# A transformer layer in three blocks: q and k of the cross-attention made transposed and packed through DRAM, two heads a step, joints filled with preparation

## The chip, the cores and the metric

One core of a Trainium2 chip. The metric is the device time of one execution in microseconds (us); several executions of each kernel give a median. One execution was also recorded by the hardware profiler. The engines are TensorE (PE, matrix products and transposes), VectorE (DVE), ScalarE (ACT), GpSimd (POOL) and SyncE (SP, which here only issues DMAs). PE writes PSUM, whose banks hold 512 fp32 words per partition.

## The reference

All in fp32, x of 8 batches of 256 rows and 512 columns. Each of three blocks adds to x a function of its layernorm.

```python
x = x + _L0_attn_ref(_layernorm(x, axis=-1), L0_attn_wqkv, L0_attn_wg, L0_attn_wo, L0_attn_gn_weight, L0_attn_gn_bias)
x = x + _L0_xattn_ref(_layernorm(x, axis=-1), ctx_1024, fside_BxSx2_0, fside_BxSx2_0, L0_xattn_Wq, ...)
x = x + _L0_ffn_ref(_layernorm(x, axis=-1), L0_ffn_gate_w, L0_ffn_expert_fc1, ...)
# block 1, retention: 8 heads of 64
scores = einsum('bhid,bhjd->bhij', xpos(q), xpos(k)) * decay
y = group_norm(einsum('bhij,bhjd->bhid', scores, v))
out = (g * tanh(softplus(g))) * y @ wo.T          # g = x @ wg.T
# block 2, cross-attention: 32 heads of 16, context 256 rows of 256
q, (k, v) = x @ Wq, split(ctx @ Wkv);  q, k = axial_rope(q, pos), axial_rope(k, pos)
out = softmax(q k^T / 4) v @ Wout + bout
# block 3, feed-forward
probs = softmax(x @ gate_w.T)                      # 8 experts, top 2
y = sum over the two experts of p * (silu(x @ fc1.T) * (x @ fc2.T)) @ proj.T            # 352 hidden
y = y + sigmoid(x @ shared_gate.T) * (silu(x @ s1.T) * (x @ s2.T)) @ shared_proj.T      # 1408 hidden
```

## The kernel before

The blocks run one after another; x stays in SBUF as `X`, 16 tiles of 128 rows. Names of tiles begin with a_, b_ or c_ by block. An fp32 product is made of three products of rounded parts (`matmul3`, L41 to L43): every operand is split into a high part (a rounded copy, mostly on ACT) and a low part (the rest, a subtraction on DVE or POOL).

**Retention** (`retention`) is a pipeline over 8 batches, written out as `body(b, ...)` for every engine. PE's body makes the scores and values of batch b and, between them, the eight chunks of products of batch b + 1 (`gemm_chunk`); chunks 6 and 7 are the gate, with rows in the partitions. The mish of the gate is transposed on PE (L261, 8 a body) and multiplied by the normalised values into z (L410), whose parts enter the output product. The product with `blk` (L251) joins the group statistics. In the last body there are no products of a next batch beside this chain.

**Cross-attention** (`cross_attention`) handles one head in a step, T = 33 steps a batch, several batches live at once: LAGS and LAGV say how many steps a head's logits and values come behind its rows. q and k are made with rows in the partitions ("r"), rotated on DVE (L873) and POOL (L1071), and written with their high and low parts into `qs`, 64 columns a head: for q high, high, low and for k high, low, high, and further columns for the maximum. 64 transposes a batch (L797, "t") turn them, and DVE (L878) and ACT (L997) copy them to qT and kT: two heads in the 128 partitions, 64 each. A head then goes: `rows` (L730, two products), row maximum on DVE (L888), every eighth head the negated maxima (L902), transposed (L801), copied, and moved by small DMAs into qT (L712); `logits` (L742), exp on ACT (L1028), every four heads `values` (L755), a copy (L1022), the turn (L762), and the division on DVE (L910, L913). Rows have two banks of rt and logits two, one head each. Then the output is transposed (L806), multiplied by Wout and added (L884). The block's start loads and splits three pieces of weights, makes the rotation's angles, and clears `qs`, `vp` and `nm` on POOL while DVE normalises the first rows (L850).

**Feed-forward** (`feed_forward`) first makes the statistics (L1371) and normalises (L1382) on DVE in four groups of four tiles, transposes (L1653), and makes the router's logits (L1672). The shared branch has 11 pieces of 128 hidden columns and four groups, 44 steps: `up(n)`, 24 products of 512 columns, and two steps later `down(n)`, 12 products, whose result DVE adds to X (L1480). SP loads pieces as they come free and fills both row tables in DRAM with zeros (L1254); beside the branch the top two are chosen, rows are ranked and scattered by indirect DMAs (L1288). Then 39 tiles of rows sorted by expert: load, transpose (L1716), two products up, the hidden values turned (L1743), one product down, rows out. POOL gathers each token's rows, first choices while the last tiles run (`early`), second ones after them (`late`, L1307), and DVE adds them (L1558).

Each engine's order is written out; semaphores alone tie the engines together.

## Time and profile before

| | us |
|---|---|
| runs | 1725.29, 1719.75, 1698.67; median 1719.75 |
| profiled execution | 1727.18, span of its instructions 1725.4 |
| PE busy | 1480.3 |
| DVE, ACT, POOL busy | 945.3, 548.5, 491.1 |
| mean granted clock of PE | 0.933 of full speed |

Busy time is the union of an engine's instructions over the whole span. The blocks have different limits, so the shares of the span say less than those of a stage. Retention ends at 382.4 us, cross-attention at 977.5, and the experts' tiles at 1687.4.

### The profile page before, as it was taken

How to read it: one execution, taken by the hardware profiler on the slowest of the kernel's cores; microseconds unless marked ns; L12 is line 12 of the kernel's file. 1: busy time of each engine (PE TensorE's matmuls, PEld its weight loads, DVE VectorE, ACT ScalarE, POOL GpSimd, SP SyncE). 2: the span in 40 equal slices, each digit the busy share in tenths (PEclk: the TensorE clock that was granted, in tenths of full speed). 3: DMA queues.
4: the chain of work that ended last, by engine and by line, in shares of the span. 5: the costliest groups of instructions: out<-in, count | busy, mean ns of one | idle time of the engine just before them, and what ended most of it. 6: DMA issues, size and time to landing. Idle time of an engine off the chain costs nothing. (4 is left out here: it accounts for less than half of the span.)

```text
span 1725.4 us, 24524 instructions
## 1 busy us (share of the span) xinstructions
PE 1480.3 (86%) x8506; PEld 1157.7 (67%) x8506; DVE 945.3 (55%) x1715; ACT 548.5 (32%) x954; POOL 491.1 (28%) x341
## 2 busy tenths in 40 slices
PE   6899999944888888888889559999999999999970
PEld 4677777733556656656665347888887879999960
DVE  5566666555676676665655375655556542222215
ACT  3222222203365565555556222111111112232310
POOL 1122222124222212212120130354124157447034
PEclk9999999966799999989889679999999999999985
DMA  6000000011000000000000390123200033353246
GB/s 262 1 1 0 0 0 0 1 36 56 2 9 2 7 7 1 7 7 1 7 1 3 112 394 34 62 102 110 79 24 31 13 128 126 132 183 126 87 122 207
DMA packets 37285, 107.05 MB, mean 62 GB/s; under 512 B 4832, under 2 KB 5984, under 8 KB 34912
## 3 DMA queue, kind: packets, MB, share of 16 engines
q1 hardware_dynamic: 30944, 71.48, 11.6%
q0 software_dynamic: 6272, 34.61, 5.6%
q8 instruction: 48, 0.79, 0.2%
q14 instruction: 21, 0.17, 0.0%
HBM read 62.30 MB, written 43.25 MB: 61 GB/s over the span
## 5 line engine op out<-in xcount | busy, mean ns | idle before, releaser
L1028 ACT ACTIVATE b_pf<-b_rt,b_zero 128x512 f32<-128x512 f32 x256 | 172.3, 686 | 139.0 <-PE b_rt L742 135.4
L888 DVE TENSOR_REDUCE b_mx<-b_rt 128x2 f32<-128x512 f32 x256 | 174.2, 687 | 63.5 <-PE b_rt L730 62.6
L1480 DVE SCALAR_TENSOR_TENSOR residual<-c_yp,c_shared,residual 128x512 f32<-128x512 f32 x176 | 127.4, 745 | 142.4 <-PE c_yp L43 136.6
L730 PE MATMUL b_rt<-b_kT,b_qT 64*128 64x256 f32 x512 | 120.3, 342 | 23.5 <-DVE b_mx L888 23.4
L41 PE MATMUL c_fc<-c_xh,c_w 128*128 128x512 f32 x352 | 137.1, 390 | 0.0
L43 PE MATMUL c_fc<-c_xh,c_w 128*128 128x512 f32 x352 | 137.0, 389 | 0.0
L42 PE MATMUL c_fc<-c_xl,c_w 128*128 128x512 f32 x352 | 137.0, 389 | 0.0
L730 PEld LDWEIGHTS b_rt<-b_kT,b_qT 64*128 64x128 f32 x512 | 74.2, 197 | 74.8 <-DVE b_mx L888 40.6
L742 PE MATMUL b_rt<-b_qT,b_kT 64*128 64x256 f32 x512 | 114.8, 322 | 9.7 <-DMA b_qT<-b_mT 9.1
L41 PE MATMUL a_gemm<-a_wh,a_xl 128*128 128x512 f32 x256 | 110.2, 430 | 4.6 <-DVE a_xl L312 3.9
L41 PE MATMUL c_fc<-c_ring,c_xTl 128*128 x312 | 105.8, 339 | 4.8 <-DVE c_xTl L1485 4.8
L1578 ACT ACTIVATE c_s<-c_fc 128x512 f32<-128x512 f32 x44 | 26.3, 598 | 239.8 <-PE c_fc L43 234.3
L42 PE MATMUL a_gemm<-a_wl,a_xh 128*128 128x512 f32 x256 | 102.5, 400 | 0.0
L43 PE MATMUL a_gemm<-a_wh,a_xh 128*128 128x512 f32 x256 | 102.4, 400 | 0.0
L42 PE MATMUL c_fc<-c_ring,c_xTh 128*128 x312 | 101.5, 325 | 0.0
L43 PE MATMUL c_fc<-c_ring,c_xTh 128*128 x312 | 101.3, 325 | 0.0
L1494 DVE TENSOR_TENSOR c_hTl<-c_eh,c_hTh 128x384 fp32r<-128x384 f32 x39 | 21.7, 558 | 145.0 <-ACT c_hTh L1602 134.8
L797 PE MATMUL b_gm<-identity,b_qs 128*128 128x128 f32 x512 | 83.8, 315 | 7.4 <-POOL b_qs L1080 7.1
L1071 POOL TENSOR_TENSOR b_rr<-b_ac,b_bs 128x256 f32<-128x256 f32 x32 | 23.4, 731 | 234.0 <-DVE b_bs L873 233.8
L742 PEld LDWEIGHTS b_rt<-b_qT,b_kT 64*128 64x128 f32 x512 | 75.9, 195 | 16.8 <-DMA b_qT<-b_mT 11.2
L1282 POOL TENSOR_TENSOR c_w<-c_wraw,c_zero 128x1536 fp32r<-128x1536 f32 x11 | 30.4, 2761 | 195.1 <-DMA c_wraw<-in_c_ws 123.8
L797 PEld LDWEIGHTS b_gm<-identity,b_qs 128*128 128x128 f32 x512 | 65.9, 161 | 25.0 <-issue 19.5
(274 smaller groups left out, 3524.8 us busy)
## 6 DMA issues: line engine op xcount, KB each, us to landing
c_eraw<-in_c_we POOLq DMA_DIRECT2D x8, 2176.0 KB, 10.0
c_xe<-c_rows_in SPq DMA_DIRECT2D x39, 256.0 KB, 3.1
c_rows_out<-c_ye SPq DMA_DIRECT2D x39, 256.0 KB, 2.0
c_rows_in<-c_xe SPq DMA_DIRECT2D x19, 512.0 KB, 9.9
c_rows_out<-c_xe SPq DMA_DIRECT2D x19, 512.0 KB, 9.9
c_wraw<-in_c_ws SPq DMA_DIRECT2D x11, 768.0 KB, 4.4
a_raw<-in_a_w SPq DMA_DIRECT2D x5, 1024.0 KB, 5.7
out<-residual SPq DMA_DIRECT2D x16, 256.0 KB
```

The source lines that it names most:

```text
L41: nc.tensor.matmul(out, ll, rh, start=start, stop=False)
L42: nc.tensor.matmul(out, lh, rl, start=False, stop=False)
L43: return nc.tensor.matmul(out, lh, rh, start=False, stop=stop)
L730: last = nc.tensor.matmul(rt[:, h % 2, t * S:(t + 1) * S], qT[r:r + 64, m, t * P:(t + 1) * P], kT[r:r + 64, m, :], start=True, stop=True)
L742: last = nc.tensor.matmul(rt[:, 2 + h % 2, j * S:(j + 1) * S], kT[r:r + 64, m, j * P:(j + 1) * P], qT[r:r + 64, m, :], start=True, stop=True)
L797: last = nc.tensor.transpose(out[:, m * P:(m + 1) * P], qs[:, which, t, c:c + P], ident[:, :])
L888: nc.vector.tensor_reduce(out=mx[:, :, h], in_=rt[:, h % 2, :].rearrange("p (t s) -> p t s", s=S), op=ALU.max, axis=AX.X).then_inc(mx_done, 1)
L1028: nc.scalar.activation(pf[:, h % 8, :], rt[:, 2 + h % 2, :], ACT.Exp, scale=XD ** -0.5, bias=zero[:, :]).then_inc(e_done, 1)
L1071: nc.gpsimd.tensor_tensor(rr[:, :, 0:8], ac[:, 0, :, :], bs[:, 1, :, :], ALU.subtract)
L1282: nc.gpsimd.tensor_tensor(w[:, k, 0, :], wraw[:, k, 1, :], zero[:, :].to_broadcast([P, PW]), ALU.add).then_inc(wh_done, 1)
L1480: nc.vector.scalar_tensor_tensor(out=X[:, t, :], in0=yp[:, (n * 4 + k) % 3, :], scalar=shared[:, t:t + 1], in1=X[:, t, :], op0=ALU.mult, o ...
L1578: nc.scalar.activation(s[:, n % 2, :], fc[:, n % 2, 0, :], ACT.Silu).then_inc(s_done, 1)
```

## The change

- **Retention.** The gate is made transposed (weights are the stationary operand, 256 columns move), so mish is not transposed. `transpose_q` stands ahead of the wait for the group statistics. In the last body the weights Wq and Wkv of the next block are loaded and split, and the table of the rotation is made and turned by 32 transposes (`turn_table`). SP writes the constant rows of `pack` and the zeros of the row tables in this block.
- **Cross-attention.** q and k are made transposed, in two halves, rotated there, and SP writes their high and low parts to the DRAM tensor `pack` and reads them back (`chunk`) into kT and qT with 50 rows a head. `qs`, its 64 transposes and 16 copies a batch are gone. A step handles two heads, T = 16: their rows fill both banks, and so do the logits; maximum and exp work on 1024 elements. The maxima are turned in the values' bank. POOL copies the values to `vp`. Each batch ends with the statistics of its final rows for the next block (`final_first`, `final_statistics`).
- **Joint to the feed-forward.** In the last body of cross-attention the first two shared pieces and the router's weights are loaded and split, and four tiles are normalised and transposed (`lead_turn`). The other twelve are normalised on ACT between the first steps.
- **Feed-forward.** The last 8 of 44 `down` are held: their hidden values are kept, their parts are made beside the expert tiles (`pair_high`, `pair_low`), and `held_down` runs behind the experts, two pieces summed in PSUM, with 16 more additions on DVE. The early gathers wait for each other, two in flight. Loads of the first rows wait for the ninth piece.

The core of the diff (some lines between the parts shown are left out):

```diff
+                if c >= 6:
+                    for m in range(2 * (c - 6), 2 * (c - 5)):
+                        o = 3 * C + m * P
+                        for k in range(KT):
+                            last = matmul3(nc, bank[:, m % 2 * S:(m % 2 + 1) * S], (wh[k][:, o:o + P], wl[k][:, o:o + P]),
+                                           (xh[:, k, :], xl[:, k, :]), k == 0, k == KT - 1)
+                    last.then_inc(gemm_done, 1)
+                    return
...
+            def turn_table():
+                pe.wait_ge(csr_done, 1)
+                for g in range(B):
+                    if g >= 2:
+                        pe.wait_ge(tab_read, g - 1)
+                    for k in range(2):
+                        for t in range(TB):
+                            last = nc.tensor.transpose(tp[:, g % 2 * 2 + k, t * P:(t + 1) * P], csr[:, k, g * TB + t, :], ident[:, :])
+                    last.then_inc(tab_mm, 1)
...
+                if nxt:
+                    transpose_q(b + 1)
+                else:
+                    turn_table()
                 pe.wait_ge(gst_done, b + 1)
                 nc.tensor.matmul(sc[:, 0, 0:2 * KT], blk[:, :], gm[:, :, :], start=True, stop=True).then_inc(gmm_done, 1)
                 if nxt:
-                    transpose_q(b + 1)
                     gemm_chunk(b + 1, 5, False)
                     transpose_k(b + 1)
                     gemm_chunk(b + 1, 6, False)
-                pe.wait_ge(mish_done, b + 1)
-                pe.wait_ge(gmm_read, b + 2)
-                for t in range(TB):
-                    for k in range(KT):
-                        last = nc.tensor.transpose(sc[:, k // 2, k % 2 * S + t * P:k % 2 * S + (t + 1) * P],
-                                                   mish[:, 2 * t + k // 2, k % 2 * P:(k % 2 + 1) * P], ident[:, :])
-                last.then_inc(tm_done, 1)
                 if after:
                     transpose_x(b + 2, False)
                 if nxt:
...
-                dve.wait_ge(tm_done, b + 1)
-                nc.vector.tensor_tensor(z[:, :, :], y[:, :, :], sc[:, :, :].rearrange("p a (b s) -> p (a b) s", s=S), ALU.mult)\
+                dve.wait_ge(mish_done, b + 1)
+                nc.vector.tensor_tensor(z[:, :, :], y[:, :, :], mish[:, :, :], ALU.mult)\
...
+            sp.wait_ge(pads, 4)
+            for which in range(2):
+                for g in range(B):
+                    sp.dma_start(pack_dram[g, which, 3 * XD:3 * XD + 2, :, :, :].rearrange("r h c (a s) -> (r h c a) s", a=TB),
+                                 fix[:, which, :]).then_inc(fix_out, 16)
+            for n in range(SLOTS):
+                for rows in row_tables:
+                    sp.dma_start(rows[n * P:(n + 1) * P, :], zero_dram).then_inc(filled, 16)
+            sp.wait_ge(gemm_done, 8 * B)
+            for n in range(2):
+                sp.dma_start(raws[:, n, :], wb_dram[1 - n, :, :]).then_inc(next_in[n], 16)
+            sp.wait_ge(fix_out, 32 * B)
...
+            def next_weights():
+                act.wait_ge(ang_done, 1)
+                for n in range(2):
+                    act.wait_ge(next_in[n], 16)
+                    nc.scalar.copy(slots[1 - n], raws[:, n, :]).then_inc(next_done, 1)
+                for k in range(2):
+                    last = nc.scalar.activation(csr[:, k, :, :].rearrange("p t (i h) -> p (t i) h", h=16),
+                                                ang[:, k, :].rearrange("p (n o) -> p n o", o=1).to_broadcast([P, NT * 8, 16]), ACT.Sin)
+                last.then_inc(csr_done, 1)
+                for g in range(B):
+                    act.wait_ge(tab_mm, g + 1)
+                    nc.scalar.copy(table[:, :, g * S:(g + 1) * S], tp[:, g % 2 * 2:g % 2 * 2 + 2, :]).then_inc(tab_read, 1)
...
-        T, LAGS, LAGV = 33, 13, 18
-        NORM, CONTEXT, ROWS = -T, 17 - T, {0: 15 - T, 1: 18 - T, 2: 21 - T, 3: 24 - T}
...
+        T, LAGS, LAGV = 16, 8, 11
+        PLAN = [(32, "w", 1, (0, 1)), (33, "w", 1, (2,)), (34, "w", 1, (3,)), (-14, "k", 0, (0,)), (-13, "k", 0, (1,)),
+                (-12, "x", 0, (0,)), (-12, "x", 1, (0,)), (-11, "k", 1, (0, 1)),
+                (-10, "q", 0, (0, 1)), (-9, "q", 0, (2,)), (-8, "q", 0, (3,)), (-8, "q", 1, (0,)), (-7, "q", 1, (1,)), (-6, "q", 1, (2, 3)),
+                (27, "o", 0, (0,)), (27, "o", 1, (0,)), (-4, "v", 0, (0, 1)), (-3, "v", 1, (0,)), (-2, "v", 1, (1,)),
+                (30, "w", 0, (0, 1)), (31, "w", 0, (2, 3))]
...
+            def rotated_out(g, n):
+                which, c = n // 2, n % 2
+                for split, done, out, terms in ((hi, rh_done, hi_out, ((0, 2), (0, 1))[which]), (lo, rl_done, lo_out, ((1,), (2,))[which])):
+                    sp.wait_ge(done, g * 4 + (n + 1))
+                    sp.sem_inc(ready, 1)
+                    for x in terms:
+                        sp.dma_start(pack_dram[g, which, x * XD:(x + 1) * XD, :, c, :].rearrange("(r i) h s -> (i h) r s", r=2),
+                                     as_f32(split[:, :, c, :])).then_inc(out[c], 16)
+
+            def chunk(g, f):
+                c = f // 2
+                if f % 2 == 0:
+                    sp.wait_ge(hi_out[c], g * 64 + 64)
+                    sp.sem_inc(ready, 1)
+                    sp.wait_ge(lo_out[c], g * 32 + 32)
+                    sp.sem_inc(ready, 1)
+                if fresh(g):
+                    sp.wait_ge(presets, 5)
+                    sp.wait_ge(wl_done, 2)
+                else:
+                    sp.wait_ge(st_mm, (g - 1) * HP + (4 * f + 4))
+                for e in range(2):
+                    at = slice(f % 2 * 8 + e, f % 2 * 8 + 8, 2)
+                    for which, packed in enumerate((kT, qT)):
+                        sp.dma_start(as_f32(packed[64 * e:64 * e + 3 * XD + 2, 4 * f:4 * f + 4, :]), pack_dram[g, which, :, at, c, :])\
+                            .then_inc(chunk_in[f], 16)
+
+            def maxima(g, k):
+                sp.wait_ge(mt_done, g * 4 + (k + 1))
+                for c in range(2):
+                    for e in range(2):
+                        row = 64 * e + 48 + c
+                        sp.dma_start(as_f32(qT[row:row + 1, 4 * k:4 * k + 4, :]),
+                                     as_f32(mT[8 * c + e:8 * c + e + 7:2, k % 2, :])).then_inc(m_moved[k % 2], 16)
...
+            def rows(g, p):
+
+                if p % 4 == 0:
+                    pe.wait_ge(chunk_in[p // 4], g * 64 + 64)
+                pe.wait_ge(mx_done, g * HP + (p + 1))
                 for t in range(TB):
-                    last = nc.tensor.matmul(rt[:, h % 2, t * S:(t + 1) * S], qT[r:r + 64, m, t * P:(t + 1) * P], kT[r:r + 64, m, :],
-                                            start=True, stop=True)
+                    for e in range(2):
+                        r = slice(64 * e, 64 * e + 3 * XD + 2)
+                        last = nc.tensor.matmul(rt[:, e, t * S:(t + 1) * S], qT[r, p, t * P:(t + 1) * P], kT[r, p, :], start=True, stop=True)
                 last.then_inc(row_mm, 1)
...
+                elif what == "k":
+                    if 0 in parts:
                         pe.wait_ge(cl_done, g + 1)
-                    for m in range(CKT):
-                        o = (2 * m + (what == "v")) * C
+                    for r in parts:
+                        for m in range(CKT):
+                            o = m * 2 * C + (2 * r + n) * P
+                            last = matmul3(nc, out[:, r * S:(r + 1) * S], (wh[:, 1, o:o + P], wl[:, 1, o:o + P]),
+                                           (ch[:, m, :], cl[:, m, :]), m == 0, m == CKT - 1)
...
+            def maximum(g, p):
+                dve.wait_ge(row_mm, g * HP + (p + 1))
+                nc.vector.tensor_reduce(out=mx[:, :, 2 * p:2 * p + 2].rearrange("p t e -> p e t"),
+                                        in_=rt[:, 0:2, :].rearrange("p e (t s) -> p e t s", s=S), op=ALU.max, axis=AX.X).then_inc(mx_done, 1)
...
+            def copy_values(g):
+                for t in range(TB):
+                    pool.wait_ge(gm_read[BANK["v", t]], uses(g, "v", t))
+                if not fresh(g):
+                    pool.wait_ge(av_done, g * 8 + 2)
+                nc.gpsimd.tensor_tensor(vp[:, :, 0:XD], vn[:, :, :].rearrange("p t (h d) -> p (t h) d", d=XD),
+                                        zero[:, :].rearrange("p (a b) -> p a b", b=1).to_broadcast([P, TB * XH, XD]), ALU.add).then_inc(v_read, 1)
...
+            def final_statistics(g, own):
+                own.step(nc.vector.bn_stats(out=fst[:, 1, :], in_=X[:, g * TB + 1, :]))
+                nc.vector.tensor_copy(spare[:, :], fst[:, 0, 0:1])
+                for t in range(TB):
+                    last = nc.vector.bn_aggr(out=fm[:, t, :], in_=fst[:, t, :])
+                own.step(last)
+                nc.vector.tensor_copy(fmean[:, bass.ts(g, TB)], fm[:, :, 0])
+                nc.vector.tensor_scalar(fvar[:, bass.ts(g, TB)], fm[:, :, 1], EPS, None, ALU.add).then_inc(fvar_done, 1)
...
+            def normalize(a, b):
+                for t in range(a, b):
+                    nc.scalar.activation(xn[t // 4][:, t % 4, :], X[:, t, :], ACT.Identity, scale=rstd[:, t:t + 1],
+                                         bias=shift_by[:, t:t + 1]).then_inc(xn_done, 1)
...
+    NOW = STEPS - 2 * G
...
+            def held_down(g):
+                if g == 0:
+                    pe.wait_ge(he_done, SLOTS)
+                elif g == 1:
+                    pe.wait_ge(ye_done, SLOTS)
+                else:
+                    pe.wait_ge(dadded, 4 * (g - 1))
+                for j in range(2):
+                    p = 2 * g + j
+                    pe.wait_ge(pl_done, p + 1)
+                    for k in range(4):
+                        a = slice(k * P, (k + 1) * P)
+                        last = matmul3(nc, sum_at(g, k), (held_high(p)[:, a], held_low(pair(p))[:, a]),
+                                       (w[j][:, 0, 2 * C:PW], w[j][:, 1, 2 * C:PW]), j == 0, j == 1)
+                        if j == 1:
+                            last.then_inc(dm_done, 1)
+                    if j == 0:
+                        last.then_inc(pm_done, 1)
...
+            for g in range(G):
+                for t in range(4 * g, 4 * g + 4):
+                    expert_sum(t, 0)
+                for k in range(4):
+                    t = 4 * g + k
+                    dve.wait_ge(dm_done, t + 1)
+                    dve.wait_ge(summed, t + 1)
+                    nc.vector.scalar_tensor_tensor(out=X[:, t, :], in0=sum_at(g, k), scalar=shared[:, t:t + 1],
+                                                   in1=X[:, t, :], op0=ALU.mult, op1=ALU.add).then_inc(dadded, 1)
+                if g == 0:
+                    pair_low(6)
+                    pair_low(7)
+            for t in range(NT):
+                expert_sum(t, 1)
```

## Rows read from the trace of the kernel before

**Rows 1.** stages: length, busy PE, PEld, DVE, ACT, POOL; clock, DMA, GB/s
```profile
57.00:346.50 289.50, 276.95 (x1501) 207.38 (x1500) 185.44 (x403) 72.64 (x118) 61.40 (x55) 1.00 0.00 0
346.50:382.40 35.90, 17.58 (x92) 12.47 (x90) 19.40 (x37) 2.97 (x5) 5.25 (x3) 0.67 0.00 1
382.40:433.40 51.00, 21.41 (x76) 15.98 (x77) 28.82 (x31) 15.77 (x20) 22.09 (x22) 0.67 0.21 78
433.40:945.20 511.80, 442.43 (x3251) 308.92 (x3250) 328.42 (x651) 277.68 (x502) 110.67 (x114) 0.94 0.02 4
945.20:977.50 32.30, 24.80 (x132) 14.93 (x130) 5.52 (x16) 11.43 (x21) 0.02 (x1) 0.68 0.00 1
977.50:1056.20 78.70, 47.50 (x213) 38.58 (x214) 51.10 (x91) 19.61 (x32) 24.41 (x15) 0.76 0.80 295
1056.20:1393.90 337.70, 336.47 (x1502) 278.83 (x1501) 201.17 (x283) 49.28 (x82) 101.26 (x53) 1.00 0.15 54
1393.90:1687.40 293.50, 277.38 (x1595) 253.17 (x1593) 81.59 (x137) 79.06 (x158) 140.59 (x51) 0.97 0.39 134
1687.40:1725.40 38.00, 0.00 (x0) 0.00 (x0) 18.83 (x28) 0.57 (x1) 20.69 (x16) 0.53 0.67 228
```

**Rows 2.** who PE waits for, 475 to 945 us: in total, times, longest
```profile
PE b_av L762 <- ACT b_at L1022: 22.0, 14, 2.3
PE b_rt L730 <- DVE b_mx L888: 18.0, 16, 1.4
PE b_gm L801 <- DVE b_nm L902: 11.4, 15, 1.4
```

**Rows 3.** timeline of PE in three places: start, duration, instructions
```profile
610.22 0.39 PE L42 MATMUL b_gm<-b_wl,b_ch 128*128 128x512 f32 x1
610.44 0.39 PE L43 MATMUL b_gm<-b_wh,b_ch 128*128 128x512 f32 x1
...
619.55 1.07 PE L755 MATMUL b_av<-b_pf,b_vp 128*32 128x256 f32 x16
620.55 1.09 PE L797 MATMUL b_gm<-identity,b_qs 128*128 128x128 f32 x8
621.58 0.38 PE L730 MATMUL b_rt<-b_kT,b_qT 64*128 64x256 f32 x1
...
621.80 0.28 PE L730 MATMUL b_rt<-b_kT,b_qT 64*128 64x256 f32 x1
...
624.55 0.50 PE L730 MATMUL b_rt<-b_kT,b_qT 64*128 64x256 f32 x2
624.89 0.40 PE L742 MATMUL b_rt<-b_qT,b_kT 64*128 64x256 f32 x2
```

**Rows 4.** timeline of DVE, the same columns
```profile
600.23 0.68 DVE L888 TENSOR_REDUCE b_mx<-b_rt 128x2 f32<-128x512 f32 x1
600.82 0.68 DVE L873 TENSOR_TENSOR b_ac<-b_gm,b_cs 128x512 f32<-128x512 f32 x1
```

**Rows 5.** the page's costliest groups: busy, mean ns, idle before
```profile
L888 DVE TENSOR_REDUCE b_mx<-b_rt 128x2 f32<-128x512 f32 x256 | 174.2, 687 | 63.5 <-PE b_rt L730 62.6
```

**Rows 6.** timeline of SP, the moves of the maxima's rows
```profile
612.29 2.44 SPq L712 DMA_DIRECT2D b_qT<-b_mT  x4
```

**Rows 7.** DMA queues: packets, MB, share; one issue: KB, us to landing
```profile
q1 hardware_dynamic: 30944, 71.48, 11.6%
q0 software_dynamic: 6272, 34.61, 5.6%
...
c_xe<-c_rows_in SPq DMA_DIRECT2D x39, 256.0 KB, 3.1
```

**Rows 8.** who PE waits for in retention's steady part, 57 to 346 us
```profile
PE a_sc L251 <- DVE a_gm L393: 7.3, 6, 1.5
```

**Rows 9.** who PE waits for, 382 to 434 and 960 to 1100 us
```profile
PE b_gm L776 <- DVE b_xn L850: 13.5, 1, 13.5
...
PE c_tp L1653 <- DVE c_xl L1389: 17.3, 4, 8.1
```

1109 lines of the change are left out of this document (623 added, 486 removed).

## The prediction

> **What bounds the kernel now.** I read the stage table first [rows 1]: nine stretches, and in each the busy time of the five engines, the granted clock of TensorE (PE) and the share of the DMA engines. The reader should see three long stages in which PE is busy nearly all the time (retention 277 of 289.5 us, the shared branch 336 of 337.7, the experts 277 of 293.5), one long stage in which it is not (cross-attention's steady part, 442 of 511.8), and five short stretches at the joints, together 236 us with PE busy for 111, mostly at a clock of 0.67 to 0.76. The time saved can come from fewer PE instructions in the long stages or from idle in the joints. Then I read who PE waits for in cross-attention [rows 2]: the copy of the values, the row maximum, the negated maximum. Each is a short wait of 1 to 2 us inside a chain between engines, not one engine that is full: VectorE (DVE) is busy 328 and ScalarE (ACT) 278 of 511.8 us.
>
> **Durations.** In the timeline of PE [rows 3] the start times of neighbouring groups give the price of one instruction. A product of 512 columns: 610.22 to 610.44, and 0.228 us when many are in a row. Sixteen value products: 619.55 to 620.55, 1.0. Eight transposes, each with its own weight load: 620.55 to 621.58, 1.02, so 0.128 each. Rows and logits products on opposite halves of the array: a pair in 0.22. Two on the same half: 624.55 to 624.89, 0.17 each. On DVE, 512 elements out of PSUM: 600.23 to 600.82, 0.60 [rows 4].
>
> **Cross-attention, a batch.** Before, PE works 442/8 = 55.3 us and the batch takes 511.8/8 = 64.0 [rows 1]. After: rows and logits, 128 products in 64 pairs that now always alternate halves, 64 x 0.22 = 14.1. Values 8 x 1.0 = 8.0. The transposed q and k: 48 + 24 products of 256 columns. No row has such a product with a full load. Half of 0.228 is 0.114; a transpose gives 0.128 with a load in it; the same-half products of 256 columns give 0.17. I take 0.128, since a transpose loads the same 128 columns, and keep 0.114 and 0.17 as ends: 9.2. v, 12 x 0.228 = 2.7; output, 24 x 0.228 = 5.5. Transposes of x and of the output, 16 x 0.128 = 2.0; of the maxima and of the values, 24, which run in twos and cost some 0.17: 4.0. The 64 transposes of packed rows are gone. Sum 45.5.
>
> DVE is busy 328.4/8 = 41.1 a batch [rows 1], most of it in 32 maxima of 0.687 [rows 5], which start 0.60 apart. After, 16 maxima of 1024 elements cost at most the same (2 x 0.60 each, 19.2). Eight of the 16 casts were its own (-4.8); the statistics for the next block are new, two passes over 512 elements at 0.6 and five small operations of at most 0.6 each (+1.2 to +4.2; I take 2.2). Sum 38.5. ACT is busy 34.7 and loses 8 casts and 4 highs; POOL (GpSimd) is busy 13.8 and gains the copy of the values and longer lows, some 5: both have room.
>
> What makes the batch longer than 45.5: both banks for rows now serve one pair, so rows of a pair can start only when the maximum of the pair before has been taken, and the same for logits and exp. A step has 2.8 us of PE work, a chain of rows, maximum and start 0.44 + 1.2 + some 0.3 of handing over, so the chain has room unless DVE has other work in that step. Adding for each of the 16 steps the longer of its PE and its DVE work gives 47. The other waits of [rows 2] stay in part: the values are still copied before they are turned, but the turn is moved a step later, behind other work. The 8.4 us of waits per batch before shrink to some 5.5. I take 51 us a batch, range 46 to 58. The first and last batches have less beside them, some 20 us in sum; so 8 x 51 - 20 = 388 against 512: **-124**.
>
> **The trip through DRAM.** Twelve writes of 256 pieces and 16 reads of 200 pieces a batch, all of 1 KB: 6272 packets, 6.4 MB. SP issues 45 DMAs, at the 0.61 us of today's row moves [rows 6] 27 of 51, waiting in a written order: a late low of q holds the maxima behind it. Each chunk is asked for four steps (some 12 us) ahead of its use, and the maxima likewise, and a 256 KB read of a table in DRAM lands in 3.1 us [rows 7], two in line in some 5, so I cost it nothing in the steady part. The cover is the DMA engines' idle (share 0.02 in the stage [rows 1]). Bounds on a packet: the hardware queue spent 0.116 x 16 x 1725/30944 = 0.103 us on each, the software queue 0.056 x 16 x 1725/6272 = 0.246 [rows 7], both for longer packets. At 0.103 on 16 engines a batch needs 40 us, at 0.246 it needs 96.
>
> If the 50-row reads run on ten engines, those ten carry 320 + 192 packets a batch, 53 us at 0.103: a rival below. This is what the Trainium skill says, page "DMA: Bandwidth & Descriptors", section "Why a DMA increments its semaphore by 16 and not by 1": the engine count is the largest number up to 16 that divides the slowest dimension, which for 50 is 10. No row here shows a read of 50 rows.
>
> **Retention.** A body loses 8 mish transposes (1.0 us), gains 48 products of 256 columns at 0.128 for 24 at 0.228 (+0.7), and q's transposes now stand ahead of the product that waited for DVE, 7.3 us in 6 bodies [rows 8]; the final z no longer waits for PE. About -1.4 a body, seven times -10. In the last body 32 transposes of the angle table with their copies stand ahead of that product, 4.1 us, of which the wait before that product [rows 8] covers about one: +3. The zero fills (78 of 256 KB, 20 MB) and the pack's constant rows run beside a stage that uses no DMA. Nothing waits for them until the block ends: nothing. Together **-7** (-14 to +5).
>
> **Joint A to B.** 51.0 us, PE busy 21.4. Gone: loading and splitting Wq and Wkv, the angles, two memsets, the transposes and casts. PE wait for the first normalised rows (13.5, [rows 9]) was VectorE beside GpSimd's memsets; two memsets stay. After: 15 us of PE work at a low clock, 12 idle, 5 for the first trip: 32, **-19** (-25 to -6). Tail of B: eight steps of two heads, then the same output: **+1**.
>
> **Joint B to C.** 78.7 us, in which PE does three `up` (24 products, 5.5 us each), four routers and 64 transposes, some 35 us at full clock; the waits on c_xn and c_xl [rows 9] are those of a block that starts with statistics. After, group 0 is ready, the other twelve tiles are normalised on ACT between ups, and the fills no longer share the engines with the weights. I leave 11 idle: **-33** (-38 to -12). The price is a few us of DVE and POOL in B's last, light batch.
>
> **Shared branch and experts.** Eight of 44 `down` (12 products, 2.74 us) leave a stage that PE fills: **-22**, one to one. In the experts' stage 16 of 293.5 us are idle, mostly at its start and where the early gathers collide with loads; the gathers are now throttled to two in flight: **-10** (-16 to 0). **Tail.** 38 us with PE empty. The held products (22 us) fit beside the late gathers; but DVE now has 48 operations of the length of [rows 5] there, 33 us, of which the first 32 must be done before the last late sums: **+2** (0 to +15).
>
> **Sum.** -124 - 7 - 19 + 1 - 33 - 22 - 10 + 2 = -212. The profiled execution is 1727.2 us (span 1725.4) and gives 1515; against the median of the runs, 1719.75, the same difference gives **1508**.
>
> **Rivals.** (a) 256-column products cost 0.17, as on one half [rows 3]: 0.042 x (72 + 48) = 5.0 a batch in both blocks, +40: 1548. For it: the same column count. Against: those are loads behind work on the same rows, and a transpose repeats at 0.128. Chance 0.15. (b) The single pair of banks runs in lockstep: each wait of [rows 2] stays, batch 58: +56, 1564; 0.15. For it: the maxima are already what PE waits for 18 us. (c) The ten engines of the reads bound the batch at 53 plus waits that no longer hide, 55: +32, 1540; 0.05. (d) The work moved into the joints and behind the experts comes back there: the B-C joint keeps 20 of its 33, the tail grows by 15, A's last body by 5: +40, 1548; 0.08. (e) Batch 46: -40, 1468; 0.10. (f) The other side: 1 KB packets are dear. Slower by 2% needs +247 us, a batch of 82: 0.16 us a packet on ten engines (512 packets), 0.21 on sixteen. At the software queue's 0.246 the batch would be 96 to 126 us and the kernel 1870 to 2110. Against: that queue's packets hold 5.5 KB each, and at 0.103 for 2.3 KB a shorter packet should cost less. Chance 0.04. (g) The change does not do what it says (the pair is not overlapped at all, little gain, within 2%): 0.02. The forecast itself: 0.41.
>
> The second place for a page: the Trainium skill, "TensorE: Matmul & The Clock Gate", section "LDWEIGHTS (loading the stationary operand)", says that the load's time goes by its columns, about 107 ns for 128. By it, a 256-column product would hide its load and cost 0.11, some -2 a batch in both blocks together, -17 us: inside the forecast's range. The trace has it nearer 0.128 for a load with 128 columns behind it.
>
> **Range.** The forecast alone is 1475 to 1545. With (a) to (e) it reaches from 1462 to 1585, leaving out (f), (g) and the far half of (b) with (a) together. Runs of one kernel here differ by 1.5%, so 2% is about what a measurement can tell from no change. Faster 0.94, within 2% 0.02, slower 0.04.
>
> **What would show it.** Right: a batch period near 51, PE busy 45 of it; products of the transposed q and k 0.128 apart; no wait of PE on a DMA into kT or qT; the joints at 32 and 45 us; experts' tail at 40 us. Wrong: PE waiting for chunk reads (c, f), a DMA share above 0.8 in cross-attention, rows waiting on the maximum in every step (b), 0.17 between q products (a), DVE sums ending long after the last gather (d).

## The result

The changed kernel takes 1468.92 us (median of four runs, 1466.68 to 1471.77); the kernel before took 1722.52 beside it. The ratio is 0.8595, with an interval from 0.8501 to 0.8689: 14% faster. A later set of runs gave 1471.37 against 1741.3, ratio 0.8461 (0.8428 to 0.8494): the kernel before differs between sets of runs, the changed one hardly. So the experiments below are read against 1469 to 1471, not by their ratio. The forecast was 1508, with a range from 1462 to 1585. The forecast alone, without its rivals, reached from 1475 to 1545, and the measured time lies 6 us below that; it is the time of rival (e), a batch of 46 us and a total of 1468, which had a chance of 0.10.

The profiled execution has a span of 1464.8 us and a mean granted clock of 0.975 (before: 1725.4 and 0.933). The stage table of the changed kernel, cut at the same events as [rows 1]: end of retention's steady part, its end, the first and the last rows products of cross-attention, its end, the fourth `up`, the end of the last `up`, the end of the last expert tile. (In [rows 1] the last three `down` lie behind the cut at the last `up`, here none does, so the shared branch and the experts are compared together.) Columns: length, busy PE, weight loads, DVE, ACT, POOL, then clock, DMA share, GB/s.

```profile
55.00:341.80 286.80, 274.54 (x1653) 213.90 (x1653) 188.48 (x407) 77.48 (x122) 63.13 (x56) 1.00 0.18 60
341.80:371.90 30.10, 14.20 (x80) 10.36 (x76) 15.75 (x33) 10.59 (x15) 12.81 (x5) 0.77 0.00 1
371.90:403.80 31.90, 16.27 (x94) 13.92 (x94) 14.89 (x20) 7.67 (x11) 18.41 (x20) 0.80 0.53 174
403.80:752.90 349.10, 322.37 (x2976) 231.10 (x2980) 285.02 (x512) 203.51 (x295) 141.13 (x131) 0.97 0.51 150
752.90:782.00 29.10, 23.19 (x188) 14.22 (x176) 9.80 (x29) 12.65 (x18) 0.71 (x1) 1.00 0.00 1
782.00:822.05 40.05, 36.59 (x180) 30.49 (x181) 14.44 (x30) 21.44 (x34) 7.34 (x6) 0.91 0.06 20
822.05:1151.30 329.25, 326.75 (x1459) 269.93 (x1457) 179.40 (x264) 48.66 (x80) 102.05 (x54) 1.00 0.15 55
1151.30:1419.30 268.00, 262.63 (x1556) 241.34 (x1557) 86.95 (x129) 81.26 (x161) 137.96 (x47) 1.00 0.41 142
1419.30:1464.80 45.50, 21.96 (x97) 17.83 (x95) 30.81 (x47) 1.83 (x3) 27.30 (x20) 0.79 0.68 220
```

| stage | before | after | difference | forecast |
|---|---|---|---|---|
| retention, start to end | 382.4 | 371.9 | -10.5 | -7 |
| joint to cross-attention | 51.0 | 31.9 | -19.1 | -19 |
| cross-attention, steady | 511.8 | 349.1 | -162.7 | -124 |
| its tail | 32.3 | 29.1 | -3.2 | +1 |
| joint to feed-forward | 78.7 | 40.1 | -38.6 | -33 |
| shared branch and experts | 631.2 | 597.3 | -33.9 | -32 |
| tail | 38.0 | 45.5 | +7.5 | +2 |
| sum | 1725.4 | 1464.8 | -260.6 | -212 |

Six of seven terms lie within 8 us of the forecast; cross-attention's steady part holds 39 of the 49 us that were missed. To see inside it, SP's loads of the context mark one batch each (timeline of SP, start and duration), and the stage table over three such batches gives their mean:

```profile
533.76 0.36 SPq L800 DMA_DIRECT2D b_craw<-in_b_ctx  x1
...
578.92 0.36 SPq L800 DMA_DIRECT2D b_craw<-in_b_ctx  x1
...
624.08 0.36 SPq L800 DMA_DIRECT2D b_craw<-in_b_ctx  x1
```

```profile
533.76:669.28 135.52, 129.72 (x1214) 93.70 (x1212) 110.89 (x210) 80.22 (x117) 54.16 (x54) 1.00 0.50 149
```

The period is 45.2 us (forecast 51). PE is busy 129.7/3 = 43.2 of it (45.5), DVE 37.0 (38.5). Only 2 us are waits; before, the waits of the list behind [rows 2] came to 8.4 a batch, and I expected 5.5. The waits of PE in the whole stage, against [rows 2] (one of 0.4 us is left out):

```profile
PE b_rt L875 <- DVE b_mx L1051: 22.0, 25, 4.9
PE b_rt L875 <- DMA weights_b<-b_pack: 6.5, 2, 6.1
PE b_rt L887 <- DMA weights_b<-b_mT: 2.3, 2, 2.1
```

The copies of the values and the negated maxima, which made up 33 us before, are gone from the list. The maximum stays, 22 us, of which 9.6 between 440 and 700 us and the rest while the pipeline fills and empties. The prices of the products, in the timeline of PE:

```profile
383.37 0.28 PE L41 MATMUL b_gm<-b_ch,weights_a 128*128 128x256 f32 x1
383.49 0.28 PE L42 MATMUL b_gm<-b_cl,weights_a 128*128 128x256 f32 x1
...
541.75 0.50 PE L875 MATMUL b_rt<-weights_b 50*128 50x256 f32 x4 [0.48 <-DVE b_mx L1051]
542.09 0.40 PE L887 MATMUL b_rt<-weights_b 50*128 50x256 f32 x4
542.42 1.07 PE L900 MATMUL b_av<-b_pf,b_vp 128*32 128x256 f32 x16
```

383.37 to 383.49 is one product of 256 columns with a full load: 0.12 us, inside my bounds of 0.114 and 0.17 and close to the 0.128 taken. From 541.75 to 542.42 run four rows products and four logits products, 0.67 us for eight. I had put them at four pairs of 0.22, 0.88, from [rows 3]. The difference, 0.21 in each of 16 steps, is 3.4 us a batch, more than the whole difference in PE's sum. The first experiments ask why. Added up by start times over the same three batches, PE's 43.2 us are rows and logits 10.6 (14.1 forecast), the 72 products of 256 columns 10.1 (9.2), the 36 of 512 columns 9.6 (8.2), values 8.2 (8.0), the 24 small transposes 2.6 (4.0) and the other 16 transposes 2.2 (2.0). So a product of 256 columns costs 0.14 in the mean of a batch: like the pairs, it is dearer at the start of a stretch than inside it.

### The profile page after: what moved, and what is told of

Read it like the earlier page. It is cut to its first block and busy times, and to the rows that moved or that the text cites. A ratio compares the mean times of both kernels' runs of the same rounds, so it can differ in the third digit from the quotient of the medians.

```text
span 1464.8 us, 24146 instructions
## 1 busy us (share of the span) xinstructions
PE 1332.3 (91%) x8442; PEld 1070.3 (73%) x8442; DVE 852.5 (58%) x1516; ACT 484.6 (33%) x755; POOL 515.9 (35%) x352
## 3 DMA queue, kind: packets, MB, share of 16 engines
q0 software_dynamic: 6272, 34.61, 6.7%
## 5 line engine op out<-in xcount | busy, mean ns | idle before, releaser
L1051 DVE TENSOR_REDUCE b_mx<-b_rt 128x4 f32<-128x1024 f32 x128 | 156.3, 1221 | 52.5 <-PE b_rt L875 52.3
L1210 ACT ACTIVATE b_pf<-b_rt,b_zero 128x1024 f32<-128x1024 f32 x128 | 142.9, 1117 | 130.7 <-PE b_rt L887 130.4
L1839 ACT ACTIVATE c_s<-c_fc 128x512 f32<-128x512 f32 x44 | 26.3, 598 | 231.8 <-PE c_fc L43 231.7
L875 PE MATMUL b_rt<-weights_b 50*128 50x256 f32 x512 | 66.8, 340 | 29.4 <-DVE b_mx L1051 22.0
L41 PE MATMUL a_gemm<-weights_a,a_xl 128*128 128x512 f32 x192 | 82.5, 430 | 4.6 <-DVE a_xl L352 3.9
L1559 POOL TENSOR_TENSOR c_ring<-c_eraw,c_zero 128x2816 fp32r<-128x2816 f32 (+1 forms) x16 | 62.9, 3929 | 53.8 <-DMA c_eraw<-in_c_we 53.8
L1561 POOL TENSOR_TENSOR c_ring<-c_eraw,c_ring 128x2816 fp32r<-128x2816 f32 (+1 forms) x16 | 78.9, 4934 | 1.3
L43 PE MATMUL a_gemm<-weights_a,a_xh 128*128 128x512 f32 x192 | 76.2, 397 | 0.0
L43 PEld LDWEIGHTS c_fc<-c_xh,c_w 128*128 128x128 f32 x352 | 66.1, 188 | 13.7
L42 PEld LDWEIGHTS c_fc<-c_xl,c_w 128*128 128x128 f32 x352 | 66.1, 188 | 13.5
L41 PEld LDWEIGHTS c_fc<-c_xh,c_w 128*128 128x128 f32 x352 | 66.1, 188 | 13.5
L900 PE MATMUL b_av<-b_pf,b_vp 128*32 128x256 f32 x1024 | 69.5, 390 | 0.0
## 6 DMA issues: line engine op xcount, KB each, us to landing
c_rows_out<-in_b_ctx SPq DMA_DIRECT2D x39, 256.0 KB, 10.1
```

The source lines that it names most:

```text
L41: nc.tensor.matmul(out, ll, rh, start=start, stop=False)
L42: nc.tensor.matmul(out, lh, rl, start=False, stop=False)
L43: return nc.tensor.matmul(out, lh, rh, start=False, stop=stop)
L875: last = nc.tensor.matmul(rt[:, e, t * S:(t + 1) * S], qT[r, p, t * P:(t + 1) * P], kT[r, p, :], start=True, stop=True)
L900: last = nc.tensor.matmul(av[r:r + VW, 0:S], vp[:, j * XH + h, :], pf[:, h % 8, j * S:(j + 1) * S], start=j == 0, stop=j == TB - 1)
L1051: nc.vector.tensor_reduce(out=mx[:, :, 2 * p:2 * p + 2].rearrange("p t e -> p e t"), in_=rt[:, 0:2, :].rearrange("p e (t s) -> p e t s", s ...
```

## Experiments: the price of a pair of products

Before, four products of opposite halves took 0.43 us; after, eight take 0.67. The order of issue differs and so do the rows (64 and 50). Three runs:

```diff
 # e1, kernel before: rows and logits over 50 partitions
-qT[r:r + 64, m, t * P:(t + 1) * P], kT[r:r + 64, m, :]
+qT[r:r + 50, m, t * P:(t + 1) * P], kT[r:r + 50, m, :]
 # e2, changed kernel: one half's products first, in rows and in logits
-                for t in range(TB):
-                    for e in range(2):
+                for e in range(2):
+                    for t in range(TB):
 # e3, changed kernel: over 64 partitions, the spare rows cleared
-                        r = slice(64 * e, 64 * e + 3 * XD + 2)
+                        r = slice(64 * e, 64 * e + 64)
```

> The kernel before, with the rows and logits products of a head over 50 partitions instead of 64 (the other 14 hold zeros). Question: why do four products of a pair of heads take 0.34 us after the change, where four on opposite halves took 0.44 before. Theory O (the order of issue makes them overlap: half 0, half 1, half 0, half 1 after the change; half 0, half 0, half 1, half 1 before): nothing changes, 0.22 a pair, batch 64.0, total within 3 us of before. Rival R (the 50 rows make them shorter): 0.17 a pair, some 19 steps a batch times 0.10, so about 2 us a batch, 15 us in all faster than before.

> The changed kernel, with both products of one head issued before both of the other, in rows and in logits. Theory O: the four products take 0.44 again instead of 0.34, 32 x 0.10 = 3.2 us of PE a batch, and as PE is nearly full there, about 2.5 to 3.2 us a batch, 20 to 26 us in all: about 1492. Should they take 0.17 each (0.68), it is 80 us. Rival R (row count): unchanged, 1469.

> The changed kernel, with rows and logits over 64 partitions, rows 50 to 63 of both halves cleared first (3.5 us more of DVE at the block's start). Theory O: four products still 0.34, total 1469 to 1473. Rival R: 0.44, 20 to 26 us slower, about 1492.

Measured: e1 1731.91 against 1724.48 for the kernel before in the same runs, and in its timeline a pair still took 0.22 (617.26 to 617.49). The 7 us more are outside what either theory gave; the profiled executions differ in the granted clock of PE, 0.92 in e1 against 0.933. e2 1471.87, with four products in 0.34 (611.43 to 611.77). e3 1473.86, four in 0.34 as well; its 3 us more are about the 3.5 us of clearing. So neither the order nor the rows are the cause: both theories fall. What was left was the mixture of rows and logits products in one stretch, or the length of the stretch.

```diff
 # e10, changed kernel: one function in place of rows(...) and logits(...)
+                for e in range(2):
+                    for t in range(TB):
+                        r = slice(64 * e, 64 * e + 3 * XD + 2)
+                        one = nc.tensor.matmul(rt[:, e, t * S:(t + 1) * S], qT[r, p, t * P:(t + 1) * P], kT[r, p, :], start=True, stop=True)
+                        r = slice(64 * (1 - e), 64 * (1 - e) + 3 * XD + 2)
+                        two = nc.tensor.matmul(rt[:, 3 - e, t * S:(t + 1) * S], kT[r, l, t * P:(t + 1) * P], qT[r, l, :], start=True, stop=True)
```

> The changed kernel, with rows and logits of a step issued as they ran before the change: a rows product of one half (moving operand from kT) beside a logits product of the other half (moving operand from qT), eight in a step. Neither the order (half 0 twice, then half 1: 0.34 as well) nor the 50 rows explained why four products take 0.34 after the change and 0.43 before. Theory M (two halves stream together only where their moving operands lie at the same place of the same tensor; mixed they take turns, 0.107 each): 0.86 a step instead of 0.67, 8 such steps a batch, 1.5 us a batch, and each rows product also waits for the logits' turn: 10 to 20 us in all, about 1483. Rival K (the 0.43 came from two halves being issued with fewer products in a row, not from the operands): 0.67 a step, under 3 us in all.

Measured: 1477.81 against 1471.37 in the same set. In the timeline of PE, L902 is the rows product, L904 the logits product:

```profile
561.52 0.38 PE L902 MATMUL b_rt<-weights_b 50*128 50x256 f32 x1
561.52 0.38 PE L904 MATMUL b_rt<-weights_b 50*128 50x256 f32 x1
561.75 0.28 PE L902 MATMUL b_rt<-weights_b 50*128 50x256 f32 x1
561.75 0.39 PE L904 MATMUL b_rt<-weights_b 50*128 50x256 f32 x2
561.87 0.28 PE L902 MATMUL b_rt<-weights_b 50*128 50x256 f32 x1
561.98 0.28 PE L904 MATMUL b_rt<-weights_b 50*128 50x256 f32 x1
561.98 0.28 PE L902 MATMUL b_rt<-weights_b 50*128 50x256 f32 x1
562.19 1.07 PE L918 MATMUL b_av<-b_pf,b_vp 128*32 128x256 f32 x16
```

The eight take 0.67 us, mixed or not: theory M falls. The starts show where the time is: the first pair takes 0.23, the two in the middle 0.12 and 0.11, the last 0.21. A stretch of two pairs, as before the change, consists of a first and a last one, 0.43; a stretch of four has two cheap ones between. The trace of the changed kernel has the same test without any edit. While the first batch fills the pipeline there are steps with rows and no logits, so with two pairs only, at a granted clock of 1.00:

```profile
418.12 0.51 PE L875 MATMUL b_rt<-weights_b 50*128 50x256 f32 x4
418.56 0.39 PE L41 MATMUL b_gm<-b_xh,weights_a 128*128 128x256 f32 x1
...
420.62 0.50 PE L875 MATMUL b_rt<-weights_b 50*128 50x256 f32 x4 [0.36 <-DVE b_mx L1051]
421.05 0.39 PE L41 MATMUL b_gm<-b_xh,weights_a 128*128 128x256 f32 x1
```

They take 0.44 and 0.43, with the order, the 50 rows and the operands of the changed kernel. So the length of the stretch sets the price: rival K. It gave two heads in a step a gain that I did not count. (Where the halves did not meet before, as in the last two of [rows 3], four products even took 0.67.) The Trainium skill, "TensorEngine Tiling (Array Packing)", section "Key Properties", says that a change of the tiling mode drains TensorE and that tiles work independently. That fits: some 0.1 us at each end of a stretch, and between them two products in the time of one (0.12). No run here separates the drain from another start cost. The run's 6.4 us more did not come from the steady batches (45.4 us each against 45.2), so K's limit of 3 us was missed for a reason beside the question. The context loads place it: the first three batches take 44.4, 44.4 and 46.4 us against 42.9, 42.4 and 45.2, 4.7 us in all, and from the last load to the last maximum it is 87.5 us against 82.9. So it came while the pipeline filled and emptied. In e10 a rows product also waits for what the logits beside it need; that this is the reason is argued only.

## Experiments: how much room lies behind PE

The forecast had two rivals in which something else would bound the batch: the single pair of banks (b) and the DMA engines (c, f). Both were lengthened on purpose.

```diff
 # e9: a further maximum, over one head, ahead of the maximum of a step
+                nc.vector.tensor_reduce(out=more[:, :, p:p + 1].rearrange("p t e -> p e t"),
+                                        in_=rt[:, 0:1, :].rearrange("p e (t s) -> p e t s", s=S), op=ALU.max, axis=AX.X)
```

> The changed kernel, with a maximum over one head's 512 elements ahead of each step's maximum of 1024 (its result unused): DVE works 0.6 us more in each of 16 steps, 35.6 + 9.6 = 45.2 us a batch against the period of 45.2, and the chain of rows, maximum and next rows becomes 0.34 + 0.3 + 1.8. Theory L (DVE and the single pair of banks are close behind PE): the batch grows by 3 to 6 us, 25 to 45 us in all. Rival S (there is slack behind PE, as the 2 us of waits a batch suggest): under 1 us a batch, under 8 us in all.

Measured: 1528.63, 57 to 60 us more. The context loads are 52.7 us apart. Three batches in the stage table:

```profile
560.47:718.51 158.04, 136.71 (x1213) 98.21 (x1212) 144.00 (x259) 81.46 (x117) 53.46 (x54) 0.96 0.43 128
```

DVE is busy 48 us a batch of 52.7, PE 45.6 instead of 43.2 for the same products, at a granted clock of 0.96 instead of 1.00: a part of the loss is the lower clock. Of the 9.6 us added to each batch, 7.5 came through. PE's waits for the maximum rose from 22.0 to 52.8 us (404 to 780 us). Rival S falls. Theory L was right in kind and too small in size: with 2 us of waits a batch the changed kernel looks free of its chain of banks, yet it is only just so. DVE's 37.0 us and the chain together carry little more before they bound the batch; the edit lengthens both, so which of the two binds is not shown.

```diff
 # e4: a copy within DRAM for each read into kT; e5: for each read into kT and qT
+                        sp.dma_start(pack2[g, which, :, at, c, :], pack_dram[g, which, :, at, c, :]).then_inc(extra, 16)
```

> The changed kernel, with 8 further DMAs a batch from DRAM to DRAM, each a copy of one read of the pack (50 rows of 4 KB in 1 KB pieces), behind that read in SP's order. In the profile after, such reads run at a DMA share of 0.55 to 0.70 and some 165 GB/s, so on ten of sixteen engines, and take 19 us a batch there, the writes 9 on all sixteen: 29 of 45. With 8 copies the ten engines carry about 38 of 45 us. Theory H (the trip is hidden, and has room): under 1 us a batch, total under 1477. Rival N (near the edge): a read lands later and PE waits for it, 2 us a batch or more, over 1485.

> The same with 16 copies a batch, as many as there are reads. The ten engines would carry 48 us of a batch of 45. Theory T (ten engines bound the reads): the batch follows them, 48 to 52 us, total 1490 to 1525, and PE waits for the reads of the pack. Rival A (all sixteen engines share the work, 29 + 12 = 41 or less): hardly any change, under 1480.

The rows on which these expectations rest are the stage table of the changed kernel in single microseconds: the first while writes of the pack run, the others while reads run.

```profile
545.50:546.50 1.00, 1.00 (x13) 0.86 (x12) 0.83 (x6) 0.41 (x1) 0.02 (x1) 1.00 1.02 339
...
565.60:566.60 1.00, 1.00 (x18) 0.42 (x16) 1.00 (x1) 0.84 (x1) 0.24 (x1) 1.00 0.65 171
566.60:567.60 1.00, 1.00 (x9) 0.55 (x5) 0.15 (x1) 0.56 (x2) 0.00 (x0) 1.00 0.65 157
```

Writes hold all engines busy at 339 GB/s; reads stay near 0.65 and 160 to 170 GB/s. 10/16 is 0.63, so the 50-row reads run on ten engines, as the prediction's sentence on the Trainium skill had it ("DMA: Bandwidth & Descriptors", section "Why a DMA increments its semaphore by 16 and not by 1"): by that rule, the trace agrees. A packet of 1 KB keeps an engine for 1.024/16.5 = 0.062 us in a read and for 0.048 in a write. My bounds of 0.103 and 0.246 were both too high, because those packets were longer. [Rows 7] held the answer: 71.48 MB in 0.116 x 16 x 1725 us is 22.3 GB/s an engine, and 34.61 MB in 0.056 x 16 x 1725 is 22.4. At that rate 1 KB takes 0.046 us, which is what the writes show; the reads are slower, for a reason that no run shows.

Measured, two runs each: e4 1489.7, 18 to 21 us more; e5 1515.0, 44 to 46 more. In e4 a batch takes 46.3 us in the mean of five, against 44.2 for the same five of the changed kernel: 2.1 more. PE waits 16.8 us in all for reads of the pack (6.5 in the changed kernel), 12.1 of it ahead of 500 us, 8.2 at once. So theory H falls, and N came as it was put: the trip is hidden with little room, least at the start. In e5 the batches take 46 to 52 us, 49.4 in the mean of six (44.3), and PE waits for both DMAs into qT and kT:

```profile
PE b_rt L879 <- DMA weights_b<-b_pack: 28.2, 17, 9.8
PE b_rt L891 <- DMA weights_b<-b_mT: 16.7, 16, 5.7
```

That is what theory T gave: 48 to 52 us, 1490 to 1525. The DMA share over these six batches is 0.63. The writes take some 9 us a batch on all sixteen engines; with them taken apart, I estimate from these rows that the ten engines are busy for 44 of 49.4 us. Had all sixteen shared the load, there would have been room for it. But a rival stands: the copies also keep SP. One takes 0.86 us to issue, a read 0.35, so in e5 SP's issues add up to 35.4 us a batch instead of 22.8, and four reads go out in 6.1 us instead of 1.8, with the moves of the maxima behind them. A read that lands late because it was asked for late looks the same to PE. The two runs show that the trip has little room; whether it is lost on the ten engines or in SP's order they do not separate.

## Experiments: the tail

The tail was the only term that came out worse by more than 3 us: 45.5 instead of 40. Two edits meet there, the throttled early gathers and the held products.

```diff
 # e6: four early gathers in flight
-                if t >= 2:
-                    pool.wait_ge(landed0[t % 2], 16 * (t // 2))
+                if t >= 4:
+                    pool.wait_ge(landed0[t % 4], 16 * (t // 4))
 # e8: nothing held
-    NOW = STEPS - 2 * G
+    NOW = STEPS
...
+            down(STEPS - 2)
             expert_up(0, 0)
             expert_up(0, 1)
+            down(STEPS - 1)
...
-            for g in range(G):
-                held_down(g)
```

In e8 `pair_high`, `pair_low` and the 16 additions of held work are gone too.

> The changed kernel, with four early gathers in flight instead of two. Now the 16 early gathers take 1396.9 to 1425.8 us, 1.8 us each, and the late ones, which could start when the last tile has landed at about 1422, start at 1427.5. Theory Q (the throttle costs the tail and protects nothing that four would hurt): gathers 1.25 us each from the start, the early ones done at 1417, the late ones start 5 us earlier, and the total falls by 4 to 6 us, to about 1464. Rival P (the gathers then delay the loads and stores of the last expert tiles, which the throttle was there to prevent): PE waits again among the last tiles, and the total stays or rises by up to 5 us.

> The changed kernel with all 44 down products at their places and none held behind the experts; the additions go with them. Theory W (held work is hidden behind the gathers): the stages up to the last tile grow by 8 x 2.74 = 22 us; the tail falls from 45.5 towards the 38 of before, since POOL's gathers no longer stand beside 16 more additions; net +14 us, about 1483. Rival V (the tail's 7.5 us more come from the throttled gathers, not from the held work): the tail stays at 45, net +22, about 1491.

e6: 1481.12, 10 to 12 us more. The early gathers go at 1.25 us each and the tail behind the last product shortens to 42.5 us, but PE waits among the last tiles:

```profile
PE c_ey L41 <- issue: 5.7, 1, 5.7
PE c_fc L41 <- DVE c_xTl L1721: 4.9, 1, 4.9
```

These are the stalls of the kernel before (10.7 us there). So the throttle pays more than it costs, and even four in flight bring the whole loss back. Theory Q falls, P holds, beyond its 5 us. e8: 1489.85, 19 to 21 us more, between W (14) and V (22). From the last router products to the last tile it takes 622 us, 24 more than in the changed kernel (22 forecast). Its tail behind the last product, by the stage table:

```profile
1446.90:1487.50 40.60, 0.15 (x1) 0.00 (x0) 19.31 (x29) 0.59 (x1) 22.10 (x20) 0.53 0.75 245
```

40.6 us instead of 45.5: of the 24 us that holding the products saves ahead of the tail, 5 are given back here. (A second profile of the changed kernel has a tail of 43.4, so differences of 2 us between tails are not clear of the noise.) A tail has three parts: from the last product to the first late gather, from the first to the last start of one, and from there to the end.

| | to the first late gather | first to last | to the end | tail |
|---|---|---|---|---|
| before | 3.0 | 23.9 | 11.1 | 38.0 |
| after | 8.2 | 26.8 | 10.5 | 45.5 |
| after, second profile | 7.3 | 26.3 | 9.8 | 43.4 |
| e6, four in flight | 3.2 | 29.3 | 10.0 | 42.5 |
| e8, nothing held | 8.5 | 19.7 | 12.4 | 40.6 |
| e11 | 7.7 | 22.3 | 14.0 | 44.0 |

So most of the 7.5 us by which the tail grew, 5.2, is the later start of the late gathers: it stays without held work (e8) and goes with four gathers in flight (e6), so it is the throttle's. That part of rival V was right. The middle part, 2.9 us longer than before and 7.1 longer than in e8, is looked at next. The tail of the changed kernel, first DVE (L1797 sums of gathered rows, L1807 additions of held work), then POOL (L1564, the gathers):

```profile
1432.19 2.72 DVE L1797 SCALAR_TENSOR_TENSOR residual<-c_early,c_gain,residual 128x512 f32<-128x512 f32 x4
1434.84 2.71 DVE L1807 SCALAR_TENSOR_TENSOR residual<-c_fc,c_shared,residual 128x512 f32<-128x512 f32 x4
1437.47 2.73 DVE L1797 SCALAR_TENSOR_TENSOR residual<-c_early,c_gain,residual 128x512 f32<-128x512 f32 x4
1440.12 2.06 DVE L1807 SCALAR_TENSOR_TENSOR residual<-c_yp,c_shared,residual 128x512 f32<-128x512 f32 x3
1442.10 0.74 DVE L1807 SCALAR_TENSOR_TENSOR residual<-c_ex,c_shared,residual 128x512 f32<-128x512 f32 x1
1442.76 5.38 DVE L1797 SCALAR_TENSOR_TENSOR residual<-c_late,c_gain,residual 128x512 f32<-128x512 f32 x8
```

```profile
1431.35 0.95 POOL L1564 DMA_INDIRECT c_late<-c_rows_out,c_rows  x1 [0.30 <-issue]
1432.60 3.13 POOL L1564 DMA_INDIRECT c_late<-c_rows_out,c_rows  x1 [0.31 <-issue]
1436.04 0.95 POOL L1564 DMA_INDIRECT c_late<-c_rows_out,c_rows  x1 [0.30 <-issue]
1437.29 0.95 POOL L1564 DMA_INDIRECT c_late<-c_rows_out,c_rows  x1 [0.30 <-issue]
1438.54 2.48 POOL L1564 DMA_INDIRECT c_late<-c_rows_out,c_rows  x1 [0.30 <-issue]
...
1443.83 5.12 POOL L1564 DMA_INDIRECT c_late<-c_rows_out,c_rows  x1 [0.30 <-issue]
```

A gather takes 0.95 us, but the one at 1432.60 ends at 1435.73, the one at 1438.54 at 1441.02, the one at 1443.83 at 1448.95. Each ends 0.8 us after a run of L1797 (1434.91, 1440.20, 1448.14) and none is held by L1807. The kernel before had one such, of 5.73 us, which ended 0.8 us after a run of sums. But not every run holds: the gather at 1427.51 took 0.95 us, wholly beside four sums that ran from 1426.90 to 1429.62. The Trainium skill, "GPSIMD Engine Reference", section "Specifications", says that GpSimd shares its SBUF interfaces with VectorE, with contention when a VectorE instruction has two SBUF inputs. L1797 has two, L1807 one and one in PSUM: by that rule, the trace agrees in the gathers that were held, and not in the one at 1427.51. A run then tested it:

```diff
 # e11: the order on DVE in the tail
             for g in range(G):
-                for t in range(4 * g, 4 * g + 4):
-                    expert_sum(t, 0)
                 for k in range(4):
                     t = 4 * g + k
+                    expert_sum(t, 0)
```

> The changed kernel, with DVE's tail in another order: one sum of an early row, then one addition of held work, in turn, instead of four and four. In the profile after, the late gathers' issue on POOL takes 0.95 us, but 3.13, 2.48 and 5.12 where it begins beside DVE's runs of sums from SBUF (L1797), never beside runs of additions from PSUM (L1807). Theory B (such a run keeps POOL's gather from ending until the run is over): single sums hold a gather for at most 0.7 us; the two longer ones beside the early sums shrink by some 3.5 us together, total 2 to 4 us less. Rival D (what holds the gathers is the queue's own space or the DMAs in flight): the same three or more stalls stay, total unchanged within 1 us.

Its gathers, and the last row of DVE:

```profile
1437.82 1.22 POOL L1564 DMA_INDIRECT c_late<-c_rows_out,c_rows  x1 [0.30 <-issue]
...
1449.93 1.20 POOL L1564 DMA_INDIRECT c_late<-c_rows_out,c_rows  x1 [0.30 <-issue]
```

```profile
1449.58 10.68 DVE L1797 SCALAR_TENSOR_TENSOR residual<-c_late,c_gain,residual 128x512 f32<-128x512 f32 x16
```

No gather is held longer than 0.3 us any more, and from the first late one to the last it is 22.3 us instead of 26.8. So theory B came true for single sums, and D, by which the stalls would stay, falls. B's wording for runs is too strong: the gather at 1449.93 lies beside the unbroken last run of sums and took 1.20 us, and in e12 three gathers beside a run of eight took 1.02 to 1.20. Which runs hold a gather is not shown. And the total is 1468.93 against 1471.37 in the same set, with ranges that overlap (1466.76 to 1472.45, 1467.08 to 1473.39), and the tail is no shorter (44.0 us). DVE ended last instead: it stood idle from 1419 to 1425 and had all late sums still ahead at 1449.58. So the last run filled that idle time.

```diff
 # e12: the order on DVE; the last four early gathers no longer wait
+            for t in range(8):
+                expert_sum(t, 0)
+            for t in range(8):
+                add_held(t)
+                if t == 3:
+                    pair_low(6)
+                    pair_low(7)
+                expert_sum(8 + t, 0)
+            for t in range(8):
+                add_held(8 + t)
+                expert_sum(t, 1)
+            for t in range(8, NT):
+                expert_sum(t, 1)
```

> The changed kernel, with the tail in the order that the last runs point to: DVE takes eight early sums at once, from 1418.7 us on, where it now stands idle for the held products; then additions of held work alternate with the other early sums and with the first eight late sums; and the last four early gathers no longer wait for each other. With the sums alternating, POOL issued all late gathers by 1451.4 and DVE ended last, 10.7 us of late sums from 1449.6 on. DVE's 48 operations of 0.72 us and two of 0.68 from 1418.7 on end at 1455 if it never waits; the last late gather lands at about 1455, its four sums take 2.7, the output some 4: the end at about 1461 in the profile, total 1464 to 1467, 3 to 5 us under 1470. If the gathers are held longer by the eight sums in a run, or the early gathers delay the last tile's rows, it is 1470 again.

Measured: 1467.83 (1464.86 to 1470.12). The late gathers now start from 1429.3 to 1448.8, 19.5 us. DVE then had a gap of 8.3 us at 1443.9, ahead of the thirteenth addition, for which the profile names no releaser that fits: PE had finished its last held product by 1445. The gain, 1 to 4 us against runs of other sets, is not clear of the ranges. What that gap waits for stays open.

## Why the prediction was right, and where its sizes were off

The stages that the change was to shorten came out shorter by about what was forecast, with cross-attention as the exception: it holds 39 of the 49 us. The total inside the range owes something to its width. Rival (e) had its time, a batch of 46, but named no cause.

- **Cross-attention's sum of PE.** 45.5 forecast, 43.2 measured. The term that was mis-sized is "64 pairs x 0.22": it took a price from stretches of two pairs, where both are edge pairs. In stretches of four a pair costs 0.67/4 = 0.17 in the mean. That is 3.4 us a batch. The small transposes were 1.4 us cheaper too, and the products of 256 and 512 columns 2.3 us dearer, so a part of the sum came right by luck.
- **256-column products.** 0.128 taken; 0.12 measured inside a stretch, 0.14 in the mean of a batch. Rival (a), 0.17, did not come.
- **Waits in a batch.** 5.5 forecast, 2 measured. I scaled the old waits down; but of the three chains in [rows 2] two were removed by the change (the turn behind other work, maxima asked for a step later), and only the maximum stayed; that these two steps removed them is the likely reason, no run undoes one of them. Step by step, my own sum of the longer of PE and DVE had given 47, nearer than the 51 that I chose. PE and waits together are 5.8 us a batch, 46.4 in eight.
- **First and last batches.** Taken as 20 us lighter; 8 x 45.2 - 349.1 = 12.5. The 7.5 us less, taken from the 46.4, leave the 39.
- **DVE.** 38.5 forecast, 37.0 measured. Rival (b), lockstep, did not come, but e9 shows it close: half a maximum more costs 57 to 60 us.
- **The trip through DRAM.** Costed at nothing. In the steady batches that came (0.7 us of waits between 440 and 700 us); over the stage PE waited 8.8 us for the two DMAs into kT and qT, most of it at the start, where "no wait" was named as a sign of being right. The cover that I named, idle DMA engines, went from a share of 0.02 to 0.51, and e4 and e5 show that half as many or as many copies again are no longer hidden. Rival (c) was right about the ten engines and wrong about the price of a packet; (f) needed 0.16 us a packet, it is 0.06. Both bounds took the time of a longer packet for that of a short one.
- **Clock.** The sum was made of prices at full clock and had no term for it. The granted clock of cross-attention's steady part rose from 0.94 to 0.97, that of the whole execution from 0.933 to 0.975. What this gave is not separated from the rest.
- **Retention.** -10.5 against -7. PE's wait for the group statistics fell from 13.4 us in seven waits to 3.7 in six over the whole block (7.3 to 2.3 in the steady part of [rows 8]), as transposing q first was to do.
- **Joints.** The first came out as forecast to 0.1 us, the second at 40 us instead of 45.7, with PE busy for 36.6.
- **Shared branch and experts.** -33.9 against -32; PE's idle time in the experts' stage fell from 16.1 us to 5.4, and e6 shows that the throttle did it.
- **Tail.** +7.5 against +2. I counted DVE's 48 operations and not the two things that came: the throttled early gathers keep the late ones back by 5.2 us, and gathers held beside sums take 2.9 us more than before. The price of the throttle was set at nothing without a reason. The bound of +15 held it.

## What to carry to other kernels

A price read from a timeline belongs to the stretch it stood in: look at the first, the middle and the last instruction of the stretch, and ask whether the change makes stretches longer. A wait that is small in the profile is no measure of the room behind it; lengthen the suspected chain on purpose and see how much comes through. When a queue is throttled to protect one stage, ask what waits for its last transfer in the next one. Turn a queue's time into GB/s an engine before you take it as the price of a packet of another length. When POOL issues indirect DMAs beside runs of DVE instructions with two SBUF operands, look for gathers that last longer than the others; breaking the runs up removed them here, but gained no time that is clear of the noise, because DVE then ended last.
